# Attention and a mixture of experts on one core: the V products of a group's second quarter in two halves, the transpose of the maxima between them, and the order of two copies on ScalarE

## The chip, the cores and the metric

The kernel runs on one core of a Trainium2 chip. The metric is device time in microseconds (us) of one execution, as the median of several. The core's engines work from queues of their own and wait for each other by semaphores: TensorE (PE for matmuls, PEld for loading their weights), VectorE (DVE), ScalarE (ACT), GpSimd (POOL), and SyncE (SP), which issues most transfers.

## What is computed

Two sequences of 512 tokens with 512 features go through a layer norm, an attention with 32 heads of 16 features, an output projection with a residual, a second layer norm, and a mixture of 8 experts of which each token takes 2. Only the attention matters here:

```python
q, k, v = (proj(w_q), proj(w_k), proj(w_v))          # 2 x 32 heads x 512 x 16
scores = jnp.einsum('bhqd,bhkd->bhqk', q, k) / jnp.sqrt(jnp.float32(D_K))
attn = jax.nn.softmax(scores, axis=-1)
out = jnp.einsum('bhqk,bhkd->bhqd', attn, v)
...
x = x + _L0_attn_ref(_layernorm(x, axis=-1), L0_attn_w_q, L0_attn_w_k, L0_attn_w_v, L0_attn_w_o)
x = x + _L0_ffn_ref(_layernorm(x, axis=-1), L0_ffn_gate_w, L0_ffn_w1, L0_ffn_w2, L0_ffn_w3)
```

## The kernel before

Each engine has its program written out by hand; nothing is scheduled by a tool. The prologue projects Q, K and V (split in a high and a low part, which `three` on lines 711 to 715 multiplies), the attention loop follows, and behind it the output projection, the router and the experts.

The attention works in 16 groups (`NG`) of 4 heads (`GH`). For a group there are four kinds of work on TensorE:

- `key_max` (line 737): 16 key products, one for each head and each 128 queries. Each fills one of three banks with scores of 128 queries against 512 keys, and VectorE takes their maximum (`maximum`, line 1399, into `neg_max`). A bank is free again when VectorE has read it (`max_bank_free`).
- `max_t` (line 731): one transpose of the group's 16 columns of maxima (`neg_max`, 128x16) into the same three banks. ScalarE copies the result to `max_rows` (`maxima`, line 1133, the copy on line 1138), and SyncE writes it as one more row of the group's `q_stack`, so that the score products subtract the maximum.
- `scores` (line 746): for each 128 keys and each pair of heads, two products (line 756) into `ps4`, the scores with keys on the partitions. ScalarE takes their exponential (line 1183) into `probs_t`, 8 such units in a group.
- `pv` (line 717): for each 128 keys `kc` and each of the 4 heads, one product of the exponentials with V (`v_ones`, 16 features, each beside a one that makes the sum) on line 725. Its 32 output rows are the head's strip of `ps_o` (`tile_position=(0, 32 * j)`). Behind the four chunks ScalarE copies `ps_o` to `o_raw` (line 1173).

The loop's round `s` interleaves three groups, in quarters `p` of 0 to 3: key products of group `s + 2`, scores of group `s`, and V products, of group `s - 1` in the first two quarters (its chunks 2 and 3) and of group `s` in the last two (its chunks 0 and 1). A quarter has two key products, then the V products, then a key product, two score products, a key product and two score products. In the second quarter (`p == 1`) the transpose `max_t(s + 1)` stands right behind the V products:

```python
                    if p < 2:
                        pv(s - 1, p + 2)
                    else:
                        pv(s, p - 2)
                    if p == 1 and s + 1 < NG:
                        max_t(s + 1)
                    key_max(ga, 4 * p + 2)
```

ScalarE goes through the 8 exponentials of group `s`; ahead of the third (`u == 2`) it copies group `s - 1`'s outputs and then group `s + 1`'s maxima. The V products of chunk 0 wait for the output copy of the group before (line 723), and an exponential waits until the V products that read its half of `probs_t` are done (line 1181).

Of the kernel before, what the change touches and what calls it, by code (L numbers as in the profile page):

```python
# [15 lines left out]
GH = 4  # L16
NG = B * NH // GH
# [26 lines left out]
def moe_layer(nc: bass.Bass, x, wq, wk, wv, wo, gw, w13, w2, w2t, out):  # L44
# [8 lines left out]
    with ctx:  # L53
        def sem(name):
            return ctx.enter_context(nc.semaphore(name))
# [197 lines left out]
        s_pv = sem("s_pv")  # L253
# [154 lines left out]
        def max_bank(g, what):  # L408
            return max_banks[turn_of[g, what] % 3]

        def max_bank_free(eng, g, what):

            n = turn_of[g, what] - 3
            if n >= 0:
                before, what = turns[n]
                if what in ("maxima", "projection", "router"):
                    eng.wait_ge({"maxima": s_mr, "projection": s_res, "router": s_t2e}[what], before + 1)
                else:
                    eng.wait_ge(s_mx, before * 16 + what + 1)
# [7 lines left out]
        def _(sp):  # L427
# [108 lines left out]
            def ahead(i):  # L536

                e, new = of_tile(i)
                for q, (_, u1) in enumerate(LOADS):
                    sp.wait_ge(s_lo13, NU * (i - 1) + u1)  # L540
                    load13(q, e, new)
                if isinstance(i, int) and i == 1:
                    for m in range(subs_of(1)):
                        sp.wait_ge(s_xg[m], 16 * (landed(1, m) + 1))
                    sp.dma_start(out[0:T, :].rearrange("(n p) h -> p n h", p=P), x1[:, :, :]).then_inc(s_init, 16)
                for h in range(3):
                    sp.wait_ge(s_lo2[h], i)
                load2(e, new)
# [161 lines left out]
        def _(pe):  # L710
            def three(o, x_hi, x_lo, w_hi, w_lo, start, stop):

                pe.matmul(o, x_hi, w_hi, start=start, stop=False)  # L713
                pe.matmul(o, x_hi, w_lo, start=False, stop=False)  # L714
                return pe.matmul(o, x_lo, w_hi, start=False, stop=stop)  # L715

            def pv(g, kc):

                if not 0 <= g < NG:
                    return  # L720
                pe.wait_ge(s_ex, UNITS * g + 2 * (kc + 1))
                if kc == 0 and g >= 1:
                    pe.wait_ge(s_or, g)
                for j in range(GH):
                    last = pe.matmul(ps_o[32 * j:32 * j + 32, :],  # L725
                                     v_ones[:, (g // 8) * TPB + kc, (g % 8) * GH + j, :, :].rearrange("p d o -> p (d o)"),
                                     probs_t[:, kc % 2, j, :], start=(kc == 0), stop=(kc == TPB - 1),
                                     tile_position=(0, 32 * j))
                last.then_inc(s_pv, 1)

            def max_t(g):

                pe.wait_ge(s_mx, 16 * (g + 1))
                max_bank_free(pe, g, "maxima")
                pe.transpose(max_bank(g, "maxima")[0:4 * GH, 0:P], neg_max[:, g % 2, :], ident[:, :]).then_inc(s_mt, 1)

            def key_max(g, u2):

                if g >= NG:
                    return  # L740
                j, qt, _ = scores_at(u2)
                q, k = head_at(g, j, ROWS)
                max_bank_free(pe, g, u2)
                pe.matmul(max_bank(g, u2), q[:, qt * P:(qt + 1) * P], k, start=True, stop=True).then_inc(s_sn, 1)  # L744

            def scores(g, u):

                if not 0 <= g < NG:
                    return
                n = g * UNITS + u  # L750
                if n >= 2:
                    pe.wait_ge(s_ex, n - 1)
                kc, half = divmod(u, 2)
                for c in range(2):
                    q, k = head_at(g, 2 * half + c, ROWS + 1)
                    last = pe.matmul(ps4[:, 2 * (n % 2) + c, :], k[:, kc * P:(kc + 1) * P], q, start=True, stop=True)  # L756
                last.then_inc(s_st, 1)

            def keep_warm(o, count):

                for _ in range(count):
                    pe.matmul(o[:, 0:2 * P], idle_b[:, 0:P], idle_b[:, :], start=True, stop=True)

            for n, (kind, b, i) in enumerate(jobs):
# [10 lines left out]
                if kind == "t":  # L775
                    pe.wait_ge(s_xn, b * TPB + i + 1)
                    for c in range(HC):
                        last = pe.transpose(o[:, c * P:(c + 1) * P], x_sb[:, b * TPB + i, c * P:(c + 1) * P], ident[:, :])
                else:
# [7 lines left out]
                    for c in range(HC):  # L787
                        x2 = [t[:, c, :] for t in (xnT_hi, xnT_lo)]
                        w2 = [t[which][:, c, :] for t in (w_hi, w_lo)]
                        if kind == "v":  # L790
                            last = three(o, *(t[:, at] for t in x2), *w2, c == 0, c == HC - 1)
                        else:
                            last = three(o, *(t[:, at] for t in w2), *x2, c == 0, c == HC - 1)
# [31 lines left out]
            def projection(t, c0, c1):  # L825

                if c0 == 0:
                    max_bank_free(pe, t, "projection")
                project(max_bank(t, "projection"), t, c0, c1)

            for s in range(0, NG + 1):
                ga = s + 2
                if ga < NG and ga % 2 == 0:
                    pe.wait_ge(s_stack[(ga // 2) % RING], 16 * 12 * (ga // 2 // RING + 1))
                if 0 <= s < NG:
                    pe.wait_ge(s_row[s % 4], 32 * (s // 4 + 1))

                for p in range(TPB):
                    no_pv = 2 - p if s == 0 and p < 2 else 0
                    key_max(ga, 4 * p)  # L840
                    keep_warm(ps_o, no_pv)
                    key_max(ga, 4 * p + 1)
                    keep_warm(ps_o, no_pv)
                    if p < 2:
                        pv(s - 1, p + 2)
                    else:
                        pv(s, p - 2)
                    if p == 1 and s + 1 < NG:
                        max_t(s + 1)
                    key_max(ga, 4 * p + 2)  # L850
                    scores(s, 2 * p)
                    keep_warm(ps_o, no_pv)
                    key_max(ga, 4 * p + 3)
                    scores(s, 2 * p + 1)
                    keep_warm(ps_o, no_pv)
                    if s in (NG - 2, NG - 1):
                        projection(s - (NG - 2), p, p + 1)
                    elif s == NG and p == 0:
                        projection(2, 0, HC // 2)
# [75 lines left out]
            for t in range(NT):  # L935
                last = pe.matmul(ps2[:, 0, 0:E], ones_b[:, :], pk[:, t * E:(t + 1) * E],
                                 start=(t == 0), stop=(t == NT - 1))
# [5 lines left out]
            for t in range(NT):  # L943
                last = pe.matmul(ps4[:, 0, 0:2], row_hot_0[:, t, :], token_of_0[:, t, :],
                                 start=(t == 0), stop=(t == NT - 1))
# [158 lines left out]
            for half, done in enumerate((s_xt_0, s_xt)):  # L1104
                for c in range(2):
                    at = slice((2 * half + c) * P, (2 * half + c + 1) * P)
                    last = pe.transpose(ps2[:, half, c * P:(c + 1) * P], xg[:, 1, at], ident[:, :])
# [13 lines left out]
        def _(a):  # L1121
# [11 lines left out]
            def maxima(g):  # L1133

                a.wait_ge(s_mt, g + 1)
                if g >= 2:
                    a.wait_ge(s_row[(g - 2) % 4], 32 * ((g - 2) // 4 + 1))
                a.activation(max_rows[:, g % 2, :], max_bank(g, "maxima")[0:4 * GH, 0:P], ACT.Copy).then_inc(s_mr, 1)
# [26 lines left out]
            for s in range(0, NG + 1):  # L1165
                for u in range(UNITS):
                    g = s - 1
                    if u == 2 and g >= 0:
                        a.wait_ge(s_pv, TPB * (g + 1))
                        if g >= 2:  # L1170
                            a.wait_ge(s_so[g % 2], 16 * (g // 2))
                            a.wait_ge(s_on, g - 1)
                        a.activation(o_raw[:, g % 2, :], ps_o[:, :], ACT.Copy).then_inc(s_or, 1)
                    if u == 2 and s + 1 < NG:
                        maxima(s + 1)
                    if 0 <= s < NG:
                        n = s * UNITS + u
                        kc, half = divmod(u, 2)
                        m = s * TPB + kc
                        if m >= 2 and half == 0:  # L1180
                            a.wait_ge(s_pv, m - 1)
                        a.wait_ge(s_st, n + 1)
                        a.activation(probs_t[:, kc % 2, 2 * half:2 * half + 2, :], ps4[:, 2 * (n % 2):2 * (n % 2) + 2, :],  # L1183
                                     ACT.Exp, scale=D ** -0.5).then_inc(s_ex, 1)
# [608 lines left out]
```

## Time and profile before

| | us |
|---|---|
| median of 3 runs | 568.57 (568.17 to 572.58) |
| the profiled execution, its own time | 568.12 |
| its span, first to last instruction | 566.3 |
| TensorE busy | 542.8 (96%) |
| VectorE busy | 390.8 (69%) |
| ScalarE busy | 323.4 (57%) |

The attention loop takes some 180 of these us. A matmul's record begins when it enters the array; its end is modelled, so records of one engine can overlap. A wait in brackets at the end of a timeline row is the idle time of that engine before the row, and what ended it. PE and PEld are two queues of one engine, and where PEld is idle, PE may be at work. The chain of waits is followed back from the last instruction and names at each moment the work that the end had to wait for.

### The profile page before, as it was taken

The page shows a single profiled execution, that of the slowest core. Times are in us where ns is not written, and L with a number is a line of the kernel's source. Part 1 is how long each engine was busy: PE and PEld are TensorE (multiplying, and loading weights), DVE is VectorE, ACT ScalarE, POOL GpSimd, SP SyncE. Part 2 cuts the span into 40 slices and gives each one's busy share as a digit, 9 for nine tenths or more (in the row PEclk, how much of TensorE's full clock was granted, in tenths as well). Part 3 has the DMA queues.
Part 4 walks back from the last instruction along what each step waited for, and adds up shares of the span by engine and source line. Part 5 has one row for each costly group of instructions (what it writes and reads, how often), then busy time and mean ns, then how long its engine had stood idle before and what let it go on. Part 6 is the DMA issues. An engine that isn't in the chain of part 4 may idle for free.

```text
span 566.3 us, 9787 instructions
## 1 busy us (share of the span) xinstructions
PE 542.8 (96%) x3520; PEld 393.4 (69%) x3520; DVE 390.8 (69%) x729; ACT 323.4 (57%) x480; POOL 127.8 (23%) x154
## 2 busy tenths in 40 slices
PE   7999999999999999999998999999999999999991
PEld 5886665333333333333677988999999999999981
DVE  6914656999999999971579987664828465566650
ACT  4322114777777777778346563747656565757540
POOL 3300111000221211451301113234340321331212
PEclk9999999999999999999999999999999999999997
DMA  8290368827557752002284499694664757486112
GB/s 325 102 111 2 51 84 90 114 40 90 74 78 94 91 74 89 21 12 87 95 316 124 148 339 341 173 331 87 236 197 136 271 148 282 93 301 167 41 30 36
DMA packets 31116, 78.19 MB, mean 138 GB/s; under 512 B 9692, under 2 KB 10972, under 8 KB 26586
## 3 DMA queue, kind: packets, MB, share of 16 engines
q1 hardware_dynamic: 25770, 68.84, 46.3%
q0 software_dynamic: 5296, 8.69, 8.1%
q8 instruction: 30, 0.49, 0.4%
q14 instruction: 20, 0.16, 0.1%
HBM read 53.11 MB, written 9.32 MB: 110 GB/s over the span
## 4 chain that ended last, share of the span: by engine, by line
PE 83%; DVE 10%; DMA 3%; issue 2%; POOL 1%; ACT 1%; POOLq 0%; DVEq 0%; ACTq 0%
PE ps L713 17%; PE ps L715 16%; PE ps L714 16%; PE ps_o L725 11%; PE ps L744 8%; DVE neg_max L1399 5%; PE ps_m L744 4%; PE ps L756 2%; DMA xn<-xn_rows,from_now 1%; PE ps_m L977 1%; PE ps_m L713 1%; PE ps_o L713 1%; DVE xnT_lo L1425 1%; PE ps_m L714 1%; PE ps_o L715 1%
## 5 line engine op out<-in xcount | busy, mean ns | idle before, releaser
L1183 ACT ACTIVATE probs_t<-ps 128x1024 f32<-128x1024 f32 x128 | 124.0, 1021 | 42.1 <-PE ps L756 42.1
L1399 DVE TENSOR_REDUCE neg_max<-ps 128x1 f32<-128x512 f32 x171 | 111.5, 682 | 10.5 <-PE ps L744 7.9
L713 PE MATMUL ps<-xgT_hi,w_hi 128*128 128x256 f32 (+7 forms) x384 | 110.6, 288 | 0.9 <-DVE xgT_lo L1657 0.8
L714 PE MATMUL ps<-xgT_lo,w_hi 128*128 128x256 f32 (+7 forms) x384 | 109.7, 286 | 0.0
L715 PE MATMUL ps<-xgT_hi,w_lo 128*128 128x256 f32 (+7 forms) x384 | 109.7, 286 | 0.0
L744 PE MATMUL ps<-k_stack,q_stack 48*128 48x512 f32 x171 | 73.0, 461 | 2.6 <-issue 0.3
L713 PEld LDWEIGHTS ps<-xgT_hi,w_hi 128*128 128x128 f32 x384 | 72.7, 189 | 1.4 <-DVE xgT_lo L1657 0.9
L714 PEld LDWEIGHTS ps<-xgT_lo,w_hi 128*128 128x128 f32 x384 | 72.7, 189 | 0.1
L715 PEld LDWEIGHTS ps<-xgT_hi,w_lo 128*128 128x128 f32 x384 | 72.7, 189 | 0.0
L725 PE MATMUL ps_o<-probs_t,v_ones 128*32 128x512 f32 x512 | 68.2, 605 | 0.0
L1674 DVE TENSOR_TENSOR act<-gate,ps 128x256 f32<-128x256 f32 (+7 forms) x48 | 20.7, 430 | 66.1 <-PE ps L715 52.8
L744 PEld LDWEIGHTS ps<-k_stack,q_stack 48*128 48x128 f32 x171 | 29.4, 183 | 50.4 <-DVE neg_max L1399 39.7
L756 PE MATMUL ps<-q_stack,k_stack 49*128 49x512 f32 x256 | 63.2, 423 | 0.3 <-ACT probs_t L1183 0.3
L1399 DVE TENSOR_REDUCE neg_max<-ps_m 128x1 f32<-128x512 f32 x85 | 58.0, 682 | 7.1 <-PE ps L744 3.8
L1500 DVE TENSOR_TENSOR w_lo<-w_sb,w_hi 128x1024 fp32r<-128x1024 f32 x48 | 56.6, 1218 | 0.0
L1257 ACT ACTIVATE gate<-ps 128x256 f32<-128x256 f32 (+7 forms) x48 | 18.8, 393 | 59.6 <-PE ps L715 59.4
L1205 ACT ACTIVATE w_hi<-w_sb 128x1024 fp32r<-128x1024 f32 x48 | 48.6, 1056 | 2.6 <-DMA w_sb<-w 2.4
L627 POOL TENSOR_TENSOR o_norm<-o_raw,rec_all 128x512 f32<-128x512 f32 x16 | 20.6, 1285 | 112.5 <-DVE rec_all L1474 112.5
L744 PE MATMUL ps_m<-k_stack,q_stack 48*128 48x512 f32 x85 | 39.0, 459 | 1.1
L756 PEld LDWEIGHTS ps<-q_stack,k_stack 49*128 49x128 f32 x256 | 30.8, 185 | 7.8 <-ACT probs_t L1183 6.5
L673 POOL DMA_INDIRECT out<-xn,to_now x20 | 33.8, 1691 | 6.2 <-issue 6.2
L744 PEld LDWEIGHTS ps_m<-k_stack,q_stack 48*128 48x128 f32 x85 | 15.6, 183 | 24.8 <-DVE neg_max L1399 19.5
(315 smaller groups left out, 990.7 us busy)
## 6 DMA issues: line engine op xcount, KB each, us to landing
w_sb<-w SPq DMA_DIRECT2D x16, 1024.0 KB, 7.1
w_sb<-w SPq DMA_DIRECT2D x8, 1536.0 KB
w_sb<-w SPq DMA_DIRECT2D x8, 1152.0 KB, 8.2
q_stack<-q_hi SPq DMA_DIRECT2D x32, 128.0 KB, 5.4
k_stack<-k_hi SPq DMA_DIRECT2D x32, 128.0 KB, 5.0
q_stack<-q_lo SPq DMA_DIRECT2D x16, 128.0 KB, 4.5
k_stack<-k_lo SPq DMA_DIRECT2D x16, 128.0 KB, 6.0
q_hi<-o_norm SPq DMA_DIRECT2D x16, 128.0 KB, 4.4
```

Source lines behind the costliest of these rows:

```text
L673: pool.indirect_dma_start(out=out[:, :], out_offset=bass.IndirectOffsetOnAxis(ap=to_now[0:rows, m:m + 1], axis=0), in_=y_sb[0:rows, m, :], ...
L713: pe.matmul(o, x_hi, w_hi, start=start, stop=False)
L714: pe.matmul(o, x_hi, w_lo, start=False, stop=False)
L715: return pe.matmul(o, x_lo, w_hi, start=False, stop=stop)
L725: last = pe.matmul(ps_o[32 * j:32 * j + 32, :], v_ones[:, (g // 8) * TPB + kc, (g % 8) * GH + j, :, :].rearrange("p d o -> p (d o)"), prob ...
L744: pe.matmul(max_bank(g, u2), q[:, qt * P:(qt + 1) * P], k, start=True, stop=True).then_inc(s_sn, 1)
L756: last = pe.matmul(ps4[:, 2 * (n % 2) + c, :], k[:, kc * P:(kc + 1) * P], q, start=True, stop=True)
L1183: a.activation(probs_t[:, kc % 2, 2 * half:2 * half + 2, :], ps4[:, 2 * (n % 2):2 * (n % 2) + 2, :], ACT.Exp, scale=D ** -0.5).then_inc(s_ ...
L1205: a.activation(w13_hi[:, at], w13_sb[:, at], ACT.Copy).then_inc(s_hi13, 1)
L1399: v.tensor_reduce(neg_max[:, g % 2, col:col + 1], max_bank(g, u2), AX.X, ALU.max, negate=True).then_inc(s_mx, 1)
L1500: v.tensor_tensor(w13_lo[:, at], w13_sb[:, at], w13_hi[:, at].bitcast(f32), ALU.subtract).then_inc(s_lo13, 1)
L1674: v.tensor_tensor(act[:, u % 2, 0:cap], gate[:, u % 2, 0:cap], ps4[:, pair + 1, 0:cap], ALU.mult).then_inc(s_act, 1)
```

## The change

In `pv` the heads become an argument, and the semaphore of the V products is raised only where the last head is among them. In the second quarter of a round the V products of heads 0 and 1 come first, then the transpose of the maxima, then the V products of heads 2 and 3. On ScalarE the copy of the maxima moves ahead of the copy of the outputs. The number of products, copies and waits for data is the same.

```diff
@@ -714,19 +714,20 @@
                 pe.matmul(o, x_hi, w_lo, start=False, stop=False)
                 return pe.matmul(o, x_lo, w_hi, start=False, stop=stop)
 
-            def pv(g, kc):
+            def pv(g, kc, heads=range(GH)):
 
                 if not 0 <= g < NG:
                     return
                 pe.wait_ge(s_ex, UNITS * g + 2 * (kc + 1))
                 if kc == 0 and g >= 1:
                     pe.wait_ge(s_or, g)
-                for j in range(GH):
+                for j in heads:
                     last = pe.matmul(ps_o[32 * j:32 * j + 32, :],
                                      v_ones[:, (g // 8) * TPB + kc, (g % 8) * GH + j, :, :].rearrange("p d o -> p (d o)"),
                                      probs_t[:, kc % 2, j, :], start=(kc == 0), stop=(kc == TPB - 1),
                                      tile_position=(0, 32 * j))
-                last.then_inc(s_pv, 1)
+                if GH - 1 in heads:
+                    last.then_inc(s_pv, 1)
 
             def max_t(g):
 
@@ -841,12 +842,14 @@
                     keep_warm(ps_o, no_pv)
                     key_max(ga, 4 * p + 1)
                     keep_warm(ps_o, no_pv)
-                    if p < 2:
+                    if p == 1 and s + 1 < NG:
+                        pv(s - 1, p + 2, range(GH // 2))
+                        max_t(s + 1)
+                        pv(s - 1, p + 2, range(GH // 2, GH))
+                    elif p < 2:
                         pv(s - 1, p + 2)
                     else:
                         pv(s, p - 2)
-                    if p == 1 and s + 1 < NG:
-                        max_t(s + 1)
                     key_max(ga, 4 * p + 2)
                     scores(s, 2 * p)
                     keep_warm(ps_o, no_pv)
@@ -1165,14 +1168,14 @@
             for s in range(0, NG + 1):
                 for u in range(UNITS):
                     g = s - 1
+                    if u == 2 and s + 1 < NG:
+                        maxima(s + 1)
                     if u == 2 and g >= 0:
                         a.wait_ge(s_pv, TPB * (g + 1))
                         if g >= 2:
                             a.wait_ge(s_so[g % 2], 16 * (g // 2))
                             a.wait_ge(s_on, g - 1)
                         a.activation(o_raw[:, g % 2, :], ps_o[:, :], ACT.Copy).then_inc(s_or, 1)
-                    if u == 2 and s + 1 < NG:
-                        maxima(s + 1)
                     if 0 <= s < NG:
                         n = s * UNITS + u
                         kc, half = divmod(u, 2)
```

On TensorE, in the second quarter of the loop's round 5, the rows before (`ps`, `ps_m` and `ps_o` are banks of PSUM; L744 are key products, L725 V products, L735 the transpose, L756 scores):

```order
L744 MATMUL ps_m<-k_stack,q_stack 128x512
L744 MATMUL ps<-k_stack,q_stack 128x512
L725 MATMUL ps_o<-probs_t,v_ones 32x512 x4
L735 MATMUL ps<-ident,neg_max 16x128
L744 MATMUL ps_m<-k_stack,q_stack 128x512
L756 MATMUL ps<-q_stack,k_stack 128x512 x2
L744 MATMUL ps<-k_stack,q_stack 128x512
L756 MATMUL ps<-q_stack,k_stack 128x512 x2
```

and the same place of the changed kernel, where lines below the edit have other numbers (L745 key products, L736 the transpose, L757 scores):

```order
L745 MATMUL ps_m<-k_stack,q_stack 128x512
L745 MATMUL ps<-k_stack,q_stack 128x512
L725 MATMUL ps_o<-probs_t,v_ones 32x512 x2
L736 MATMUL ps<-ident,neg_max 16x128
L725 MATMUL ps_o<-probs_t,v_ones 32x512 x2
L745 MATMUL ps_m<-k_stack,q_stack 128x512
L757 MATMUL ps<-q_stack,k_stack 128x512 x2
L745 MATMUL ps<-k_stack,q_stack 128x512
L757 MATMUL ps<-q_stack,k_stack 128x512 x2
```

The run of four V products has become two runs of two, and the transpose stands between them; nothing else has moved. On ScalarE, the same round and the next, before (L1173 copies the outputs, L1138 the maxima, L1183 are the exponentials):

```order
L1183 ACTIVATE probs_t<-ps 128x1024 x8
L1173 ACTIVATE o_raw<-ps_o 128x512
L1138 ACTIVATE max_rows<-ps_m 16x128
L1183 ACTIVATE probs_t<-ps 128x1024 x8
L1173 ACTIVATE o_raw<-ps_o 128x512
L1138 ACTIVATE max_rows<-ps 16x128
```

and in the changed kernel (L1178 outputs, L1141 maxima, L1186 exponentials):

```order
L1186 ACTIVATE probs_t<-ps 128x1024 x8
L1141 ACTIVATE max_rows<-ps_m 16x128
L1178 ACTIVATE o_raw<-ps_o 128x512
L1186 ACTIVATE probs_t<-ps 128x1024 x8
L1141 ACTIVATE max_rows<-ps 16x128
L1178 ACTIVATE o_raw<-ps_o 128x512
```

Between the same two runs of exponentials the two copies have changed places.

## Rows read from the trace of the kernel before

**Rows 1.** The profile's page: span, then busy us, share and instructions of each engine.
```profile
span 566.3 us, 9787 instructions
PE 542.8 (96%) x3520; PEld 393.4 (69%) x3520; DVE 390.8 (69%) x729; ACT 323.4 (57%) x480; POOL 127.8 (23%) x154
```

**Rows 2.** Chain of waits, second quarter of one round: start us, us, what.
```profile
150.63 0.70 DVE neg_max L1399
...
151.37 0.50 PE ps L744
151.87 1.00 PE ps_o L725 x8
152.87 0.21 PE ps L735
153.08 0.45 PE ps_m L744
```

**Rows 3.** Timeline of VectorE there: start us, us, what, count, idle before.
```profile
153.54 0.69 DVE L1399 TENSOR_REDUCE neg_max<-ps_m 128x1 f32<-128x512 f32 x1 [0.43 <-PE ps_m L744]
```

**Rows 4.** One group: us, busy us (instructions) of each engine, granted clock, DMA, GB/s.
```profile
152.80:164.15 11.35, 11.09 (x69) 4.30 (x65) 10.64 (x20) 8.50 (x11) 1.28 (x1) 1.00 0.65 84
```

**Rows 5.** Timeline of ScalarE around the two copies.
```profile
152.94 0.60 ACT L1173 ACTIVATE o_raw<-ps_o 128x512 f32<-128x512 f32 x1
153.43 0.25 ACT L1138 ACTIVATE max_rows<-ps 16x128 fp32r<-16x128 f32 x1
153.85 1.94 ACT L1183 ACTIVATE probs_t<-ps 128x1024 f32<-128x1024 f32 x2 [0.17 <-PE ps L756]
```

**Rows 6.** Timeline of TensorE's matmuls, second quarter and the next.
```profile
151.80 1.07 PE L725 MATMUL ps_o<-probs_t,v_ones 128*32 128x512 f32 x8
152.80 0.28 PE L735 MATMUL ps<-ident,neg_max 128*16 128x128 f32 x1
153.01 0.50 PE L744 MATMUL ps_m<-k_stack,q_stack 48*128 48x512 f32 x1
...
153.82 0.41 PE L744 MATMUL ps<-k_stack,q_stack 48*128 48x512 f32 x1
...
154.72 1.06 PE L725 MATMUL ps_o<-probs_t,v_ones 128*32 128x512 f32 x8
155.72 0.50 PE L744 MATMUL ps<-k_stack,q_stack 48*128 48x512 f32 x1
```

**Rows 7.** Line 725 alone in three stretches: us, PE busy, PEld busy, clock, DMA, GB/s.
```profile
151.80:151.82 0.03, 0.02 (x4) 0.02 (x4) 1.00 2.36 246
152.25:152.28 0.03, 0.03 (x8) 0.00 (x0) 1.00 0.00 0
151.83:152.25 0.42, 0.42 (x4) 0.13 (x8) 1.00 0.93 98
```

**Rows 8.** Timeline of TensorE, a run of eight transposes behind the loop.
```profile
291.80 1.03 PE L867 MATMUL ps<-ident,xn 128*128 128x128 f32 x8
```

**Rows 9.** Timeline of weight loads: the transpose, and two key products behind it.
```profile
152.80 0.09 PEld L735 LDWEIGHTS ps<-ident,neg_max 128*16 128x16 f32 x1 [0.84 <-DVE neg_max L1399]
...
153.73 0.18 PEld L744 LDWEIGHTS ps<-k_stack,q_stack 48*128 48x128 f32 x1 [0.19 <-ACT max_rows L1138]
154.29 0.18 PEld L744 LDWEIGHTS ps_m<-k_stack,q_stack 48*128 48x128 f32 x1 [0.37 <-DVE neg_max L1399]
```

**Rows 10.** Line 1138 (the maxima's copy): who waited for it (us, times).
```profile
PEld ps L744: 1.5, 8
PEld ps_m L744: 0.9, 5
```

**Rows 11.** Chain of waits, the last round with a transpose.
```profile
253.37 1.00 PE ps_o L725 x8
254.37 0.21 PE ps L735
```

## Prediction

> **What bounds the kernel now.** I read the profile's page first, then the chain of waits of one steady group of the attention loop, then the timeline of each engine around the place that the change touches.
>
> The page shows a kernel that is almost full on TensorE, 542.8 of 566.3 us, with VectorE and ScalarE at 69% and 57% [rows 1]. Such shares do not tell what an edit in one place is worth, so the chain of waits comes next [rows 2]. In a steady group it goes round the same circle at every one of the four quarters: VectorE takes a maximum (0.70 us), which frees a bank; TensorE starts the quarter's second key product (0.50); behind it stand the V products of line 725 (1.00); then, in the second quarter only, the transpose of line 735 (0.21); then the quarter's third key product (0.45); and with that VectorE's next maximum. The reader should see that the V products lie on this path with their whole length. VectorE cannot work ahead over them, because the maxima have three banks and TensorE fills no new one while V products run: behind the second quarter's V products and transpose VectorE stands idle for 0.43 us [rows 3]. One group lasts 11.35 us, at a granted clock of 1.00, TensorE's upper level [rows 4]. ScalarE is not on the path there: before the exponentials behind the two copies it is idle for 0.17 us, until TensorE's scores come [rows 5].
>
> **What the change does on TensorE.** Before, one second quarter reads: V products start at 151.80, transpose at 152.80, third key product at 153.01 [rows 6]. From the V products' start to the key product that VectorE waits for it is 153.01 − 151.80 = 1.21 us.
>
> The question is what two heads cost instead of four. A run of line 725 is four products, one for each head, and the trace has eight records of it [rows 6], so each product runs as two passes. Cutting the run into stretches [rows 7] shows how: four matmuls have begun in the first 0.02 us; no other begins until 152.25, and the next four are there in the 0.03 us behind that. So all four heads make their first pass together, on four strips of 32 output rows, and then their second pass together. The run is long because each pass streams 512 columns, and not because there are four heads. Two heads alone must stream the same two passes of the same 512 columns: I take 1.00 us for a half run, as for a whole one.
>
> The second half can begin only when the transpose lets it. What I need is the distance from the transpose to a V product behind it, which the trace of before does not have. The nearest rows: from the transpose to a key product 0.21 us [rows 6]; eight transposes in a row take 1.03 us, so one occupies the array for (1.03 − 0.28)/7 = 0.11 us, where 0.28 is the length of a single one [rows 6, 8]; a lone key product keeps the V products behind it waiting from 151.37 to 151.80, 0.43 us [rows 2, 6]. Zero would hold if the second half could begin beside the transpose. I take 0.21, the row of the same transpose with the same array emptying behind it, and keep 0 and 0.43 as ends.
>
> From the V products' start to the third key product the changed kernel then needs 1.00 (first half, as from 151.80 to 152.80) + 0.21 (transpose) + 1.00 (second half, as from 154.72 to 155.72, where a key product follows at once [rows 6]) = 2.21 us. The difference is 2.21 − 1.21 = **1.00 us per split group**.
>
> Does the transpose really stand between the halves, rather than beside them? The weights of the second passes were loaded while the first passes ran (all eight loads lie before 152.25 [rows 7]), whereas the transpose's own load starts only at 152.80, together with its matmul [rows 9]. The transpose has no strip named in its call, and it waited until the products had run out. I read that as a barrier, so the same will hold behind it. The Trainium skill, TensorEngine Tiling (Array Packing), Key Properties, says that changing the tiling mode drains TensorE; the trace agrees with that reading, since the 0.21 us behind the transpose exceed its 0.11. The same list also says that tiles operate independently; if the transpose's 16 columns counted as one more strip, that sentence would apply instead, and it is the rival "beside" below.
>
> **How often.** Of the 16 transposes one stands in the prologue and one in the loop's first round, where no V products of an earlier group exist; the order of TensorE's instructions has 14 split runs. In 13 of them key products follow and the circle above applies (13 is also the number of waits for the copied maxima, 8 + 5 [rows 10]). In the fourteenth there are no key products left, but there the chain runs through TensorE alone, V products 1.00 and transpose 0.21 included [rows 11]. So all 14 pay in full: 14 × 1.00 = 14.0 us.
>
> **What the change moves on ScalarE.** The copy of the maxima (0.25 us) goes ahead of the copy of the outputs (0.60) and runs while the second half computes. What it removes is the wait of the third key product behind the transpose for the maxima's bank: 0.19 us in front of a weight load at 153.73, whose matmul starts at 153.82 [rows 6, 9]. Over 13 groups that is 1.5 + 0.9 = 2.4 us [rows 10]. I cost it at nothing, because the next key product waits 0.37 us for VectorE at 154.29 [rows 9]: a product that starts 0.19 earlier only makes that wait longer. Without that cover it would be a gain of 2.4 us at most.
>
> Nothing new should be late on ScalarE. The second half would run from 153.01 to 154.08; the output copy begins 0.07 behind it, as before (152.94 [rows 5] behind 152.87, where the record of the V products ends [rows 6]), and ends near 154.75. The exponential for which the scores arrive at 153.85 now [rows 5] would start at 154.85. The next group's V products, which wait for that output copy, move from 154.72 to 155.72. The row of maxima that SyncE then copies is needed only in the next round. The cover is thin, 0.10 us, and if it failed, each 0.1 us would cost 1.4 us in all.
>
> **The sum.** The profiled execution took 568.12 us (span 566.3 [rows 1]), and the median of the three runs shown is 568.57, 0.45 above it. 568.1 + 14.0 = **582.1 us**, 2.5% slower. Everything behind the attention only starts later.
>
> **Rivals.**
> - *Cheap restart*: the second half begins beside the transpose (distance 0). A group pays 1.00 − 0.21 = 0.79, the sum 11.1: 579.2 us. For it: only 16 of the columns are the transpose's. Against it: its late weight load. Chance 0.07.
> - *Dear restart*: the second half waits as long as V products do behind a lone key product, 0.43. A group pays 1.22, the sum 17.1: 585.2 us. For it: that row. Against it: half of it is the key product's own 512 columns, where the transpose has 128. Chance 0.05.
> - *Beside* (not slower): the two later heads, on strips that nobody uses, overtake the transpose and run beside the first two, so that TensorE needs 1.21 us as before. Then the change costs nothing, and it may gain the 2.4 us of the bank's wait if the weight load there decides: 565.7 to 568.1 us. It decides if the transpose occupies only its strip. For it: passes of different heads do run together [rows 7]. Against it: the transpose's load at 152.80. Chance 0.05.
> - *Price by heads* (no change): a pass of two heads takes half the time of four, 0.25, so both halves together still take 1.00: 568.1 us. For it: no row has a run of two heads. Against it: the four begin together and none follows another. Here the Trainium skill, TensorE: Matmul & The Clock Gate, Part 3, bears out the row: a packed run lasts as one matmul plus about 4 ns for each further tile. Chance 0.03.
>
> **How the numbers follow.** The likeliest case has 0.80, and with it alone I would say 581 to 584 us. The range reaches to both restart cases, 579.0 to 585.5, and leaves out the last two rivals, 0.08. A measurement of this kernel can tell about 1% from no change, 5.7 us. Slower by more than that are the first three cases, 0.92; the other two are within 1%, 0.07 with 0.01 kept for an unseen gain over 1%.
>
> **What would show it.** In the changed profile line 725 should stand in two stretches of four records of about 1.07 us with the transpose between them, the second starting 0.21 us behind the transpose; the third key product 2.2 us behind the first V product; VectorE's idle stretch there 1.4 us instead of 0.43; a group of 12.35 us instead of 11.35; no wait for the copied maxima; the maxima's copy ahead of the output copy; and no change in the stages behind. A second half that begins before the transpose ends, or runs of 0.5 us, would prove me wrong.

## The result and the profile after

The changed kernel takes 581.63 us (median of 4 runs, 581.22 to 582.30), the kernel before, run beside it, 568.87. The ratio is 1.0217 with a 95% interval of 1.0193 to 1.0241: the change costs 2.2%, 12.8 us.

The page of the changed kernel, as [rows 1]:

```profile
span 579.4 us, 9787 instructions
PE 556.5 (96%) x3520; PEld 395.4 (68%) x3520; DVE 390.7 (67%) x729; ACT 325.2 (56%) x480; POOL 127.9 (22%) x154
```

The span is 13.1 us longer. The number of instructions is the same on every engine. VectorE is as busy as before, ScalarE 1.8 us busier, and TensorE 13.7 us busier, with the same 3520 matmuls. Its own share of the span is 96% in both, so the share says nothing of the loss.

TensorE's matmuls around the second quarter, as [rows 6] (start us, us, engine, line; the key products are L745 here and the transpose L736):

```profile
155.23 0.50 PE L745 MATMUL ps<-k_stack,q_stack 48*128 48x512 f32 x1
155.66 1.05 PE L725 MATMUL ps_o<-probs_t,v_ones 128*32 128x512 f32 x4
156.64 0.28 PE L736 MATMUL ps<-ident,neg_max 128*16 128x128 f32 x1
156.85 1.05 PE L725 MATMUL ps_o<-probs_t,v_ones 128*32 128x512 f32 x4
157.83 0.49 PE L745 MATMUL ps_m<-k_stack,q_stack 48*128 48x512 f32 x1
```

Four records of line 725 now last as long as eight did: 1.05 us against 1.07. From the first V product to the third key product it is 157.83 − 155.66 = 2.17 us, where it was 1.21. The chain of waits takes both halves and the transpose in, as [rows 2]:

```profile
155.23 0.50 PE ps L745
155.73 0.98 PE ps_o L725 x4
156.71 0.21 PE ps L736
156.92 0.98 PE ps_o L725 x4
157.90 0.44 PE ps_m L745
158.34 0.02 issue
158.36 0.70 DVE neg_max L1402
```

VectorE at that place, as [rows 3], then one group from transpose to transpose, as [rows 4], and VectorE's waits in the steady part (108.8 to 268; total us, times, longest):

```profile
158.36 0.69 DVE L1402 TENSOR_REDUCE neg_max<-ps_m 128x1 f32<-128x512 f32 x1 [1.40 <-PE ps_m L745]
```

```profile
156.64:168.95 12.31, 12.03 (x67) 4.39 (x65) 10.64 (x20) 8.63 (x11) 1.28 (x1) 1.00 0.60 77
```

```profile
DVE neg_max L1402 <- PE ps L745: 14.5, 18, 1.4
DVE neg_max L1402 <- PE ps_m L745: 6.7, 9, 1.4
```

The group is 12.31 − 11.35 = 0.96 us longer, VectorE has the same 10.64 us of work in it, and its idle stretch has grown from 0.43 to 1.40 by the same amount. ScalarE, as [rows 5]:

```profile
156.95 0.27 ACT L1141 ACTIVATE max_rows<-ps 16x128 fp32r<-16x128 f32 x1 [0.23 <-PE ps L736]
157.95 0.60 ACT L1178 ACTIVATE o_raw<-ps_o 128x512 f32<-128x512 f32 x1 [0.73 <-PE ps_o L725]
158.66 1.02 ACT L1186 ACTIVATE probs_t<-ps 128x1024 f32<-128x1024 f32 x1
```

The maxima's copy does run during the second half, and nobody waits for it any more (line 1141 has no waiter in its view, where [rows 10] had 13). That is what the change set out to do; what it is worth by itself, copies_only and split_only below ask.

### The profile page after: what moved, and what is told of

It is laid out like the page before. It is cut to its first block, busy times and chain, and to the rows that moved or that the text cites. A ratio compares the mean times of both kernels' runs of the same rounds, so it can differ in the third digit from the quotient of the medians.

```text
span 579.4 us, 9787 instructions
## 1 busy us (share of the span) xinstructions
PE 556.5 (96%) x3520; PEld 395.4 (68%) x3520; DVE 390.7 (67%) x729; ACT 325.2 (56%) x480; POOL 127.9 (22%) x154
## 4 chain that ended last, share of the span: by engine, by line
PE 83%; DVE 9%; DMA 2%; issue 2%; POOL 1%; ACT 1%; POOLq 0%; DVEq 0%; ACTq 0%
PE ps L713 16%; PE ps L715 15%; PE ps L714 15%; PE ps_o L725 13%; PE ps L745 8%; DVE neg_max L1402 5%; PE ps_m L745 4%; PE ps L757 2%; DMA xn<-xn_rows,from_now 1%; PE ps_m L980 1%; PE ps_m L713 1%; PE ps_o L713 1%; DVE xnT_lo L1428 1%; PE ps_o L715 1%; PE ps_m L714 1%
## 5 line engine op out<-in xcount | busy, mean ns | idle before, releaser
L1186 ACT ACTIVATE probs_t<-ps 128x1024 f32<-128x1024 f32 x128 | 124.0, 1022 | 41.4 <-PE ps L757 39.8
L725 PE MATMUL ps_o<-probs_t,v_ones 128*32 128x512 f32 x512 | 82.7, 605 | 0.0
L745 PE MATMUL ps<-k_stack,q_stack 48*128 48x512 f32 x171 | 72.7, 460 | 2.8 <-issue 0.3
L745 PEld LDWEIGHTS ps<-k_stack,q_stack 48*128 48x128 f32 x171 | 29.1, 184 | 56.7 <-DVE neg_max L1402 48.6
L757 PE MATMUL ps<-q_stack,k_stack 49*128 49x512 f32 x256 | 63.2, 423 | 0.2 <-ACT probs_t L1186 0.2
L745 PE MATMUL ps_m<-k_stack,q_stack 48*128 48x512 f32 x85 | 38.8, 457 | 1.2
L757 PEld LDWEIGHTS ps<-q_stack,k_stack 49*128 49x128 f32 x256 | 30.8, 185 | 8.9 <-ACT probs_t L1186 6.4
L745 PEld LDWEIGHTS ps_m<-k_stack,q_stack 48*128 48x128 f32 x85 | 15.6, 184 | 27.8 <-DVE neg_max L1402 23.7
```

Of the source, the lines that this page charges most:

```text
L725: last = pe.matmul(ps_o[32 * j:32 * j + 32, :], v_ones[:, (g // 8) * TPB + kc, (g % 8) * GH + j, :, :].rearrange("p d o -> p (d o)"), prob ...
```

## The experiments

The theory: two heads cost a whole run, because a run lasts as long as its two passes over 512 columns, and the transpose separates the halves, so that the group has two runs one behind the other. Rivals: the cut as such costs; the copies' order matters; the halves would be apart whatever stands between them.

**no_gap.** Both halves are called one behind the other, and the transpose stands behind them; the copies are in the old order.

```diff
                         pv(s - 1, p + 2, range(GH // 2))
-                        max_t(s + 1)
                         pv(s - 1, p + 2, range(GH // 2, GH))
+                        max_t(s + 1)
```

> The V products are still issued in two halves, but the transpose stands behind the second half, and ScalarE's copies are in the old order. Theory (the transpose between the halves is the price): four heads run together again, a run takes 1.00 us, the time is that of the kernel before, 568.9 us within 1. Rival (the cut itself costs, by the second call's own wait or a second start): up to 0.97 us in 14 groups as in the changed kernel, 581.6 us.

Measured: 568.98 us against 568.93, ratio 0.9996 (0.9975 to 1.0018). The chain of waits has one run of eight records again:

```profile
151.77 1.00 PE ps_o L725 x8
152.77 0.21 PE ps L736
```

So cutting the call costs nothing. What stands between the halves does.

**copies_only.** TensorE's program is that of before; only ScalarE's two copies change places.

```diff
+                    if u == 2 and s + 1 < NG:
+                        maxima(s + 1)
                     if u == 2 and g >= 0:
...
-                    if u == 2 and s + 1 < NG:
-                        maxima(s + 1)
```

> Only ScalarE's two copies change places; TensorE's program is that of before. The maxima's copy can begin only behind the transpose, so the output copy moves back by some 0.7 us and the exponential behind it by some 0.4. Theory: VectorE and TensorE set the group, the exponentials have cover, 568.9 us within 1. Rival: the later exponential reaches the path and costs 0.1 to 0.4 us in 14 groups, 570 to 574 us.

Measured: 568.78 us against 568.93, ratio 0.9986 (0.9974 to 0.9998). ScalarE's timeline:

```profile
151.00 1.94 ACT L1183 ACTIVATE probs_t<-ps 128x1024 f32<-128x1024 f32 x2 [1.09 <-PE ps L756]
153.19 0.27 ACT L1138 ACTIVATE max_rows<-ps 16x128 fp32r<-16x128 f32 x1 [0.25 <-PE ps L735]
153.36 0.57 ACT L1175 ACTIVATE o_raw<-ps_o 128x512 f32<-128x512 f32 x1
153.92 1.94 ACT L1183 ACTIVATE probs_t<-ps 128x1024 f32<-128x1024 f32 x2
```

In the kernel before, the exponentials ahead of the copies started here (its copies stand in [rows 5]):

```profile
150.94 1.94 ACT L1183 ACTIVATE probs_t<-ps 128x1024 f32<-128x1024 f32 x2 [1.09 <-PE ps L756]
```

From these exponentials to the output copy it is now 153.36 − 151.00 = 2.36 us instead of 152.94 − 150.94 = 2.00, and to the next exponentials 2.92 instead of 2.91. I had expected 0.7 and 0.4 us of delay; it was 0.36 and 0.01: besides its wait for the transpose, the maxima's copy holds the output copy up for 0.17 us only (153.36 − 153.19), and the exponentials behind no longer have the 0.17 us of waiting for scores that [rows 5] shows. A gain of 0.1%, if it is one, is all that this half of the change brings, and the traces do not show it in the attention loop: the first and the last V product start at 98.7 and 274.5 us in this kernel as in the kernel before.

**split_only.** The other half alone: TensorE's program of the changed kernel, the copies in the old order.

```diff
-                    if u == 2 and s + 1 < NG:
-                        maxima(s + 1)
                     if u == 2 and g >= 0:
...
+                    if u == 2 and s + 1 < NG:
+                        maxima(s + 1)
```

> The halves with the transpose between them, but ScalarE copies the outputs first, as before. Theory: the whole price is TensorE's, 581.6 us as the changed kernel; the maxima's copy now comes behind the second half and the key product that needs its bank may wait 0.1 to 0.2 us, which lies in front of a wait for VectorE and costs nothing, at most 14 x 0.2 = 2.8 us. Rival (the copies' order gave something back that hid part of the price): 583 to 585 us.

Measured: 583.15 us, ratio 1.0247 (1.0224 to 1.0270). That is 1.5 us above the changed kernel by the medians, in the range of the rival (583 to 585 us), but against the changed kernel's 1.0217 the intervals overlap, so a gain from the copies' order is possible and not shown. The traces leave little room for it: from the first V product to the last it is 288.2 − 98.7 = 189.5 us here and 287.9 − 98.7 = 189.2 in the changed kernel, 0.3 us in the whole loop. In a steady group there is none: the second half starts 156.90 − 155.71 = 1.19 us behind the first, as in the changed kernel (156.85 − 155.66), and a key product that starts late does not move the one behind it:

```profile
155.71 1.05 PE L725 MATMUL ps_o<-probs_t,v_ones 128*32 128x512 f32 x4
156.69 0.28 PE L736 MATMUL ps<-ident,neg_max 128*16 128x128 f32 x1
156.90 1.05 PE L725 MATMUL ps_o<-probs_t,v_ones 128*32 128x512 f32 x4
...
158.79 0.50 PE L745 MATMUL ps<-k_stack,q_stack 48*128 48x512 f32 x1
159.16 0.49 PE L745 MATMUL ps_m<-k_stack,q_stack 48*128 48x512 f32 x1
```

The last two in the changed kernel:

```profile
158.63 0.40 PE L745 MATMUL ps<-k_stack,q_stack 48*128 48x512 f32 x1
159.11 0.50 PE L745 MATMUL ps_m<-k_stack,q_stack 48*128 48x512 f32 x1
```

The key product that needs the maxima's bank starts 3.08 us behind the first V product (158.79 − 155.71), in the changed kernel 2.97 (158.63 − 155.66); the next one 3.45 in both. This is the cover that the prediction named: VectorE sets that one.

**strip.** The changed kernel, with the transpose as an ordinary product with the identity, whose call names the strip of head 0.

```diff
-                pe.transpose(max_bank(g, "maxima")[0:4 * GH, 0:P], neg_max[:, g % 2, :], ident[:, :]).then_inc(s_mt, 1)
+                pe.matmul(max_bank(g, "maxima")[0:4 * GH, 0:P], neg_max[:, g % 2, :], ident[:, :], start=True, stop=True,
+                          tile_position=(0, 0)).then_inc(s_mt, 1)
```

> The changed kernel, with the transpose as an ordinary product with the identity on the strip of head 0 (the call names the strip); the program's order is the same, the halves with this product between them. Theory (the transpose takes the whole array and is a barrier): without the barrier heads 2 and 3 run beside heads 0 and 1, the group needs about 1.0 us for all four and 0.1 to 0.3 for the product behind head 0, 568 to 571 us. Rival (whatever stands between the halves in the program separates them, or two heads cost the time of four wherever they stand): 581 us.

Measured: 570.27 us against 568.93, ratio 1.0026 (0.9991 to 1.0061). The order of the program is that of the changed kernel, and all but 1.3 of its 12.8 us are gone. The profiled execution was one of the longer ones, 575.61 us: the granted clock was 0.50, TensorE's lower level, from 94.30 to 108.05 us of its span, behind a microsecond in which TensorE was busy throughout. The rows below stand in a later stretch at 1.00. TensorE's timeline, then line 725 alone in two stretches (us, PE busy and records that run in it, PEld busy), then one group:

```profile
157.76 1.33 PE L725 MATMUL ps_o<-probs_t,v_ones 128*32 128x512 f32 x8
158.65 0.38 PE L736 MATMUL ps<-ident,neg_max 128*16 128x128 f32 x2
159.02 0.50 PE L746 MATMUL ps_m<-k_stack,q_stack 48*128 48x512 f32 x1
```

```profile
157.76:157.80 0.04, 0.04 (x2) 0.04 (x4) 1.00 1.46 154
158.03:158.06 0.03, 0.03 (x4) 0.02 (x2) 1.00 1.27 137
```

```profile
158.65:170.05 11.40, 11.12 (x73) 4.50 (x67) 10.64 (x20) 8.52 (x11) 1.28 (x1) 1.00 0.66 84
```

Heads 0 and 1 start at 157.76, heads 2 and 3 at 158.03, while the first two are still in their first pass, and the product that stands between them in the program follows at 158.65, on its own strip. From the first V product to the key product it is 159.02 − 157.76 = 1.26 us. So neither the cut nor the program's order made the price: with a transpose between them the halves run one behind the other, with a product on a strip beside each other. The edit changes two things at once, the transpose into an ordinary product and the whole array into a named strip; which of the two lets the halves run together is not shown. The 0.27 us by which the later heads lag is the wait of the product for its bank: VectorE reads that bank until 157.89 here, and `ahead` below shows the same wait with the transpose. It leaves the group 0.05 us longer than before, 0.7 us in 14 groups; the rest of the 1.3 is within the interval.

**three_one.** The changed kernel, cut behind the third head.

```diff
-                        pv(s - 1, p + 2, range(GH // 2))
+                        pv(s - 1, p + 2, range(GH - 1))
                         max_t(s + 1)
-                        pv(s - 1, p + 2, range(GH // 2, GH))
+                        pv(s - 1, p + 2, range(GH - 1, GH))
```

> The changed kernel, cut behind the third head instead of the second: three heads, transpose, one head. Theory (a run costs its two passes, however many heads are in it, but for some 7 ns by which each further head starts later): a run of three takes 0.99 us, a run of one 0.98, the group is as long as in the changed kernel within 0.02, 581.6 us. Rival (the price goes by heads): three would take 0.75 of a whole run and one 0.25, 569 us; and if two heads had been dear for a reason of their own, anything else than 581.6.

Measured: 582.84 us, ratio 1.0226 (1.0165 to 1.0287).

```profile
172.03 0.99 PE ps_o L725 x6
173.01 0.21 PE ps L736
173.22 0.97 PE ps_o L725 x2
174.20 0.44 PE ps L745
```

In the chain of waits a run of three heads takes 0.99 us, a run of one head 0.97, where two took 0.98 and four 1.00. One head costs nearly what four cost: a run has a price, and a further head adds 0.01 us. The group is 12.30 us.

**ahead.** The transpose stands ahead of all four V products, which stay one run; the copies are in the new order.

```diff
-                        pv(s - 1, p + 2, range(GH // 2))
                         max_t(s + 1)
-                        pv(s - 1, p + 2, range(GH // 2, GH))
+                        pv(s - 1, p + 2)
```

> The transpose stands ahead of all four V products, which stay in one run; ScalarE copies the maxima first, as in the changed kernel. Theory (only the cut run is dear): the transpose must now wait for its bank, which VectorE is still reading, some 0.2 to 0.3 us behind the point at which the V products could start, and that wait falls on the path: 14 x 0.2 to 0.3, 571 to 573 us, far below the changed kernel. Rival (the transpose close to the V products is dear wherever it stands): 575 us or more.

Measured: 571.51 us against 568.68, ratio 1.0064 (1.0025 to 1.0103).

```profile
164.08 0.50 PE L745 MATMUL ps_m<-k_stack,q_stack 48*128 48x512 f32 x1
164.77 0.27 PE L736 MATMUL ps<-ident,neg_max 128*16 128x128 f32 x1 [0.19 <-DVE neg_max L1401]
164.97 1.06 PE L725 MATMUL ps_o<-probs_t,v_ones 128*32 128x512 f32 x8
165.97 0.50 PE L745 MATMUL ps<-k_stack,q_stack 48*128 48x512 f32 x1
```

The transpose starts 0.69 us behind the key product, where V products start 0.43 behind it [rows 2, 6]: it waits for VectorE to read its bank. The 0.26 us fall on the path, and a group takes 11.60 us (11.35 + 0.25). The maxima reach ScalarE earlier than in the changed kernel, at a quarter of its price, and still at a loss.

**strip_behind** and **strip_f32r.** Two attempts to beat the kernel before. Both leave all four V products in one run with the maxima's product behind it. The first is the kernel before with the call of `strip`; the second also keeps `neg_max` and a copy of the identity in the rounded 32-bit format.

```diff
-        neg_max = sb(ctx, "neg_max", [P, 2, 4 * GH])
+        neg_max = sb(ctx, "neg_max", [P, 2, 4 * GH], f32r)
+        ident_r = sb(ctx, "ident_r", [P, P], f32r)
...
+            a.activation(ident_r[:, :], ident[:, :], ACT.Copy).then_inc(s_ident_r, 1)
```

> The kernel before, with the transpose as an ordinary product on the strip of head 0, behind all four V products. Theory: two passes of 0.11 us behind head 0 take the place of the 0.21 of the transpose, but the array need not run empty ahead of it, so a group is 0.00 to 0.05 us shorter: 568 to 569 us. Rival (the product's two passes cost more than the barrier): 569.5 to 571.

> As strip_behind, but maxima and identity are kept in the rounded 32-bit format, in which a product has one pass instead of two (the maxima are rounded to it in the copy anyway); a copy of the identity is made at the start. Theory: 0.1 us less in each of 15 groups than with two passes, 566.5 to 567.5 us, faster than both kernels by 0.2 to 0.4%. Rival (change of format empties the array just as the transpose does): 568.9.

Measured: 568.71 us, ratio 0.9997 (0.9971 to 1.0024), and 568.20 us, ratio 0.9997 (0.9980 to 1.0015). Neither can be told from the kernel before, and the 566.5 to 567.5 us expected of the second were missed. TensorE in the first and in the second (V products L725 and L727, the maxima's product L735 and L739):

```profile
163.51 1.06 PE L725 MATMUL ps_o<-probs_t,v_ones 128*32 128x512 f32 x8
164.39 0.38 PE L735 MATMUL ps<-ident,neg_max 128*16 128x128 f32 x2
164.70 0.49 PE L745 MATMUL ps<-k_stack,q_stack 48*128 48x512 f32 x1
```

```profile
162.84 1.07 PE L727 MATMUL ps_o<-probs_t,v_ones 128*32 128x512 f32 x8
163.83 0.23 PE L739 MATMUL ps<-ident_r,neg_max 128*16 128x128 f32 x1
164.00 0.50 PE L749 MATMUL ps<-k_stack,q_stack 48*128 48x512 f32 x1
```

On the strip the product starts 0.88 us behind the V products instead of the transpose's 1.00. I read the 0.12 as the array running empty ahead of a transpose, which no row shows by itself. The product then pays most of that back by its two passes; from the V products to the key product it is 1.19 us instead of 1.21. In the rounded format it has one pass but starts 0.99 behind, as late as the transpose, and its weight load starts only there (163.83), where the first load in strip_behind stands 0.43 ahead of the product (163.96 against 164.39). I had expected 0.1 us a group less than with two passes, and it gave 0.03 (1.16 instead of 1.19). Why a product in this format starts as late as the transpose, although its call names a strip, stays open: no row tells on which part of the array it ran.

## Why the prediction was right

**The price of a half** was its main step, and it held. Without a row that showed fewer than four heads, the prediction read the price off the passes that start together [rows 7]. The changed kernel has 0.98 us for a half of two heads, three_one 0.99 for a run of three and 0.97 for a run of one. The 1.00 taken for each half was 0.02 too much, as a run is a little shorter the fewer heads start in it.

**The transpose as a barrier** was an inference from its late weight load [rows 9]. The distance from the transpose to the second half was taken as 0.21 us, from the key product behind a transpose [rows 6], and it is 156.85 − 156.64 = 0.21. The bracket at that load in [rows 9] names VectorE, a rival reading that the prediction passed over: the transpose might have waited for VectorE and not for the array. `ahead` rules it out: there VectorE holds the transpose only until 0.69 us behind the key product, which in [rows 2] would be 152.06, and it started at 152.80. That the transpose is what keeps the halves apart is shown by strip, where a product on one strip in the same place lets them run together. Both restart rivals (0 and 0.43 us) are out, "beside" does not occur with a transpose, and "price by heads" fell with three_one.

**The number of groups that pay** held: 14. In the 13 with key products VectorE's waits rose from 5.8 + 2.8 us (the same view of before, over 108.8 to 254.2) to 14.5 + 6.7, that is by 12.6 us or 13 × 0.97. In the fourteenth the chain runs through TensorE alone, as [rows 11]:

```profile
265.93 0.98 PE ps_o L725 x4
266.91 0.21 PE ps L736
267.12 0.98 PE ps_o L725 x4
```

**What was costed at nothing** was nothing. The wait for the maxima's bank is gone, and the key product behind it still starts when VectorE frees its bank (split_only shows the two products apart). The cover of 0.10 us on ScalarE was enough: the output copy begins at 157.95, 0.05 behind the second half's end at 157.90, and the exponentials at 158.66, 0.83 us behind the third key product (157.83), where it was 0.84 before (153.85 − 153.01).

**The sum** was 14 × 1.00 = 14.0 us; the trace gives 14 × 0.96 = 13.4, the span 13.1, the medians 12.8. The first difference is the 0.02 in each half. The loop accounts for all of the 13.4: from the first V product to the last it is 189.2 us instead of 175.8. The other differences are smaller than what single runs of the kernel before differ by (their spans lie between 565.6 and 572.7 us). That the predicted 582.1 us lies only 0.5 from the measured 581.63 is in part luck: the difference was 1.2 us too large, and the 568.1 that it was added to lies 0.8 below the 568.87 measured beside the change.

## What to carry to other kernels

Here products that share the array on different strips have one price for the run, 0.97 us for one head and 1.00 for four, with two passes of 512 columns each (no run changed the columns). Before cutting such a run, price each piece as the whole, and put nothing between the pieces beside which they cannot run, as here the transpose. A wait that a change removes is worth the time that the instruction behind it starts earlier at the engine that sets the pace: here 0.19 us in 13 groups stood in the list of waits, and none of it lay on the path. A small operation can be moved for nothing only to a place where both its buffer and the engine are free; here the buffer was late ahead of the run, the array was shared within it, and behind it the transpose cost its 0.21 us, the least of the three places.

## What the runs showed of the hardware

In strip, products on different strips did not start in the order of the program: the maxima's product stands ahead of heads 2 and 3 there, and started at 158.65, 0.62 us after them, when head 0 had left its strip. The Trainium skill, TensorE: Matmul & The Clock Gate, Part 3, has matmuls start strictly in program order; this trace does not agree, for products on different strips. By that order heads 2 and 3 could not have begun before 158.65, and from the first V product to the key product it would have been 0.89 + 0.98 = 1.87 us (an estimate from this run's 158.65 − 157.76 and a half run of the changed kernel) instead of the 1.26 measured.

strip_behind shows that a plain product with the identity on a strip can replace a transpose of 16 columns: its two passes last 0.38 us against the transpose's 0.28, and it starts 0.88 us behind the V products instead of 1.00.
